# A transformer tower on one core: values', maxima's and query/key work reordered in the back end of each half, biases as a weight row, maxima taken in pairs

## The reference

```python
h = layer_norm(emb_word[ids] + emb_pos)
for l in range(4):                       # "token layers"
    q, k, v = h @ Wq + bq, h @ Wk + bk, h @ Wv + bv     # 12 heads of 16
    a = band_attention(q, k, v, mask)    # tokens within +-64
    h = layer_norm(h + a @ Wo + bo)
    h = layer_norm(h + gelu(h @ W1 + b1) @ W2 + b2)
# then one causal layer with rotary q/k, a shared expert, and top-2 of 16 experts
```

## Time and profile before

| | |
|---|---|
| median of 3 runs | 7051.08 us (7049.91 to 7069.48) |
| the profiled execution | 7050.01 us, its span 7048.2 us |
| mean granted TensorE clock | 0.939 |
| busy over the span | PE 86%, DVE 60%, ACT 32%, POOL 16% |
| token layers | from about 170 to 4640 us of the span |
| causal layer | from about 4640 to 5860 us |
| choice and experts | from there to the end |

### The profile page before, as it was taken

The page is one execution under the profiler, slowest core; times in us unless marked ns, Lnnn a source line. Parts: engine busy times, 40 slices in busy tenths (PEclk is TensorE's granted clock), DMA queues, the critical chain, the costliest instruction groups (busy, mean ns, idle before and its releaser), DMA issues. The chain is left out here.

```text
span 7048.2 us, 128877 instructions
## 1 busy us (share of the span) xinstructions
PE 6042.4 (86%) x46786; PEld 4744.2 (67%) x46786; DVE 4250.6 (60%) x11172; ACT 2239.1 (32%) x4196; POOL 1101.6 (16%) x1089
## 2 busy tenths in 40 slices
PE   1999999999999999999999999978888883289999
PEld 0777777777777777777777777756666662266766
DVE  6666666666666666666666666666666664722222
ACT  0333333333333333334333333323333330011111
POOL 5011111111111111111111111111111110234333
PEclk9999999999999999999999999989999986699999
DMA  6322223323232322222332232332222320033322
GB/s 119 62 60 60 60 61 65 70 61 66 58 64 60 75 61 60 60 60 60 67 70 61 62 65 60 65 69 56 62 64 63 64 56 10 1 84 73 88 69 55
DMA packets 1204450, 441.09 MB, mean 63 GB/s; under 512 B 1050338, under 2 KB 1191044, under 8 KB 1204324
## 3 DMA queue, kind: packets, MB, share of 16 engines
q1 hardware_dynamic: 1176676, 402.69, 26.7%
q0 software_dynamic: 27648, 36.72, 3.4%
HBM read 124.23 MB, written 60.26 MB: 26 GB/s over the span
## 5 line engine op out<-in xcount | busy, mean ns | idle before, releaser
L673 ACT ACTIVATE pT<-bank 128x384 f32<-128x384 f32 x1920 | 907.9, 490 | 872.8 <-PE bank L511 872.8
L843 DVE TENSOR_REDUCE mx<-bank 128x2 f32<-128x384 f32 x1548 | 802.2, 554 | 322.0 <-PE bank L483 285.1
L582 PE MATMUL bank<-hT,w 96*128 96x256 f32 x3072 | 848.0, 442 | 85.9 <-ACT hT L688 85.9
L582 PEld LDWEIGHTS bank<-hT,w 96*128 96x128 f32 x3072 | 678.6, 224 | 236.2 <-ACT hT L688 118.2
L509 PE MATMUL bank<-maskb,eyeb 128*128 128x384 bf16 x1920 | 635.1, 331 | 78.6 <-ACT pT L673 73.3
L481 PE MATMUL bank<-maskb,eyeb 128*128 128x384 bf16 x1932 | 634.5, 328 | 39.9 <-DMA qkT<-stack 20.7
L483 PE MATMUL bank<-qkT 128*128 128x192 bf16 (+2 forms) x3864 | 636.5, 247 | 0.0
L511 PE MATMUL bank<-qkT 128*128 128x192 bf16 (+2 forms) x3840 | 630.9, 246 | 0.0
L993 DVE TENSOR_TENSOR hout<-bank,resid 128x384 f32<-128x384 f32 x128 | 71.3, 557 | 769.4 <-PE bank L594 769.4
L594 PE MATMUL bank<-w,pT 128*128 128x192 f32 x3072 | 520.4, 326 | 0.0
L1022 POOL TENSOR_TENSOR rstd<-ve,half 128x2 f32<-128x2 f32 x160 | 127.7, 798 | 2486.6 <-DVE ve L749 2486.6
(11 more groups left out here) (197 smaller groups left out, 10230.5 us busy)
## 6 DMA issues: line engine op xcount, KB each, us to landing
hcur<-hbuf SPq DMA_DIRECT2D x165, 192.0 KB, 2.4
hbuf<-hout SPq DMA_DIRECT2D x128, 192.0 KB, 2.0
amb<-am_d SPq DMA_DIRECT2D x131, 128.0 KB, 2.9
exp_wg<-in_ewg SPq DMA_DIRECT2D x16, 768.0 KB
exp_wu<-in_ewu SPq DMA_DIRECT2D x16, 768.0 KB
exp_wd<-in_ewd SPq DMA_DIRECT2D x16, 576.0 KB
xs<-xr SPq DMA_DIRECT2D x32, 272.0 KB, 2.2
hbuf<-emb_z SPq DMA_DIRECT2D x17, 384.0 KB
```

The source lines that it names most:

```text
L582: last = nc.tensor.matmul(bank[s][f // 2][:, (f % 2) * S:(f % 2 + 1) * S], w1[:, c, f * P:(f + 1) * P], hT[s][:, c, :], start=(c == 0), st ...
L673: ph.inc(nc.scalar.activation(pT[s][:, h % NPT, :], bank[s][h % 2][:, 0:SCOLS], ACT.Exp, scale=SCALE), "p", s)
L843: last = nc.vector.tensor_reduce(mx[s][:, :, h], src[:, 0:SCOLS].rearrange("p (t k) -> p t k", t=T), AX, ALU.max)
```

## The change

TensorE's order after the scores is now: hidden transposes (into bank 0 of the stream, after the fifth pair of maxima), unkept, output, **V's values** (into bank 0 of F's stream), attention transposes, **the first bank of maxima** (bank 3), projection, q/k product (banks 1 and 2), **the second and third bank of maxima** (bank 0, and bank 2 of K's stream), h1's transposes, up- and down-projection; the up-projection's fifth block (third in the causal layer) waits for all row copies. The first scores use four banks in turn and VectorE reduces two heads in one instruction. The biases of q, k and v are a 97th row of the weights, with a row of ones below the hidden state, so nothing is added behind the product: ScalarE copies the values, and in the token layers the upper bf16 part of q/k straight from PSUM to `stack` (`act_top`), VectorE only takes the difference (`dve_rest`); in the causal layer ScalarE copies q/k. VectorE's row copies are split the same way as the maxima.

```diff
-        bank = [[ctx.enter_context(nc.psum_tensor(f"bank{s}{i}", [P, 512], F32)) for i in range(4)] for s in ST]
-        wqk = sb("wqk", [DC, 2, 2 * D], F32)
-        wv = sb("wv", [DC, 2, D], F32)
+        banks = [ctx.enter_context(nc.psum_tensor(f"banks{s}", [P, 4, 512], F32)) for s in ST]
+        bank = [[banks[s][:, i, :] for i in range(4)] for s in ST]
+        wqk = sb("wqk", [DC + 1, 2, 2 * D], F32)
+        wv = sb("wv", [DC + 1, 2, D], F32)
...
         def pe_hidden_T(ph, pe, G, F, causal):
             s = G.s
             if F:
-                ph.wait(pe, "y" if causal else "r2", F.s, F.it, 0)
+                ph.wait(pe, "mx", F.s, F.it, 5)
             ph.wait(pe, "x0" if causal else "h_in", s, G.it)
-            ph.inc(pe_transposes((h1 if causal else hcur)[s], bank[s][3]), "hT_ps", s)
+            ph.inc(pe_transposes((h1 if causal else hcur)[s], bank[s][0]), "hT_ps", s)
...
         def pe_qk(ph, pe, G, F):
             if F:
-                ph.wait(pe, "mT", F.s, F.it)
+                ph.wait(pe, "mx", F.s, F.it)
...
-                    last = nc.tensor.matmul(bank[s][t][:, 0:2 * D], hTa[s][:, c, t * P:(t + 1) * P],
-                                            wqk[:, c, :], start=(c == 0), stop=(c == 1))
+                    last = nc.tensor.matmul(bank[s][1 + t][:, 0:2 * D], hTa[s][rows_of(c), c, t * P:(t + 1) * P],
+                                            wqk[rows_of(c), c, :], start=(c == 0), stop=(c == 1))
...
         def pe_scores1(ph, pe, F, h, masks, qcols, causal):
-            if h >= 3:
-                ph.wait(pe, "mx", s, F.it, h - 2)
-            dst = bank[s][h % 3]
+            if h == 3:
+                ph.wait(pe, "y" if causal else "r2", s, F.it, 0)
+            if h >= 4 and h % 2 == 0:
+                ph.wait(pe, "mx", s, F.it, h // 2 - 1)
+            dst = bank[s][h % 4]
...
+        def maxima_bank(F, f):
+            return (bank[F.s][3], bank[F.s][0], bank[1 - F.s][2])[f]
+        def pe_maxima(ph, pe, F, V, K, f):
+            s = F.s
+            if f == 0:
+                ph.wait(pe, "m", s, F.it)
+            if f == 1 and V:
+                ph.wait(pe, "v", V.s, V.it)
+            if f == 2 and K:
+                ph.wait(pe, "att", K.s, K.it)
+            dst = maxima_bank(F, f)[:].bitcast(BF16)
...
             if K:
                 pe_output(ph, pe, K)
-            if F:
-                pe_maxima(ph, pe, F)
+            if V:
+                pe_v(ph, pe, V, G, F)
             if K:
                 pe_att_T(ph, pe, K)
-            if V:
-                pe_v(ph, pe, V, G)
+            if F:
+                pe_maxima(ph, pe, F, V, K, 0)
             if K:
                 pe_project(ph, pe, K)
             if G:
                 pe_qk(ph, pe, G, F)
+            if F:
+                pe_maxima(ph, pe, F, V, K, 1)
+                pe_maxima(ph, pe, F, V, K, 2)
             if K:
                 pe_h1_T(ph, pe, K, xr if causal else h1)
                 for f in range(FSC if causal else FC):
+                    if F and f == (2 if causal else 4):
+                        ph.wait(pe, "mT", F.s, F.it)
                     (pe_shared_up if causal else pe_up)(ph, pe, K, f)
...
+        def act_v(ph, act, V, K, causal):
+            s = V.s
+            ph.wait(act, "v_ps", s, V.it)
+            if K:
+                ph.wait(act, "otT_ps", K.s, K.it)
+                if not causal:
+                    ph.wait(act, "u_ps", K.s, K.it)
+            ph.inc(nc.scalar.copy(vaug[s][:, :, :, 0:DH],
+                                  bank[1 - s][0][:, 0:2 * D].rearrange("p (t h d) -> p t h d", t=T, h=NH)), "v", s)
+        def act_top(ph, act, G):
+            s = G.s
+            ph.wait(act, "xp", s, G.it, 0)
+            for t in range(T):
+                ph.wait(act, "qk_ps", s, G.it, t + 1)
+                ph.inc(nc.scalar.copy(stack[s][:, t].rearrange("p s h (m d) -> p (s h) m d", d=DH)[:, :, 0, :],
+                                      bank[s][1 + t][:, 0:2 * D].rearrange("p (x d) -> p x d", d=DH)), "qh", s)
...
             if G:
                 ph.wait(act, "hT_ps", G.s, G.it)
-                ph.inc(nc.scalar.copy(hTa[G.s][:], bank[G.s][3][0:DC, :]), "hT", G.s)
+                ph.inc(nc.scalar.copy(hTa[G.s][0:DC], bank[G.s][0][0:DC, :]), "hT", G.s)
+            if V:
+                act_v(ph, act, V, K, causal)
             if K:
                 ph.wait(act, "aT_ps", s, K.it)
                 ph.inc(nc.scalar.copy(hT[s][:], bank[s][3][0:DC, :]), "aT", s)
+            if G:
+                (act_qk if causal else act_top)(ph, act, G)
...
+        def dve_rest(ph, dve, G):
+            s = G.s
+            for t in range(T):
+                ph.wait(dve, "qh", s, G.it, t + 1)
+                ph.inc(nc.vector.tensor_tensor(
+                    rem[s][:, t].rearrange("p s h d -> p (s h) d"),
+                    bank[s][1 + t][:, 0:2 * D].rearrange("p (x d) -> p x d", d=DH),
+                    stack[s][:, t].rearrange("p s h (m d) -> p (s h) m d", d=DH)[:, :, 0, :], ALU.subtract), "qk", s)
...
             if qcols is BAND_COLS:
-                last = nc.vector.tensor_reduce(mx[s][:, :, h], src[:, 0:SCOLS].rearrange("p (t k) -> p t k", t=T),
-                                               AX, ALU.max)
+                last = nc.vector.tensor_reduce(mx[s][:, :, at].rearrange("p t h -> p h t"),
+                                               src[:, :, 0:SCOLS].rearrange("p h (t k) -> p h t k", t=T), AX, ALU.max)
...
             if F:
-                dve_maxima_rows(ph, dve, F)
-            if V:
...
-                dve_v(ph, dve, V)
+                dve_maxima_rows(ph, dve, F, (0,))
...
-            if G:
-                dve_qk(ph, dve, G)
+            if F:
+                dve_maxima_rows(ph, dve, F, (1, 2))
+            if G and not causal:
+                dve_rest(ph, dve, G)
...
-                    sp.dma_start(vqk[:], a["vec"][bass.ds(l, 1), 0:2 * D].to_broadcast([P, 2 * D])).then_inc(w_qk, 16)
...
-                    sp.dma_start(vv[:], a["vec"][bass.ds(l, 1), 2 * D:3 * D].to_broadcast([P, D])).then_inc(w_v, 16)
```

More of the change, by code:

```diff
@@ L466, in pe_v @@
                 for c in range(2):
-                    last = nc.tensor.matmul(bank[1 - s][3][:, t * D:(t + 1) * D], hTa[s][:, c, t * P:(t + 1) * P],
-                                            wv[:, c, :], start=(c == 0), stop=(c == 1))
+                    last = nc.tensor.matmul(bank[1 - s][0][:, t * D:(t + 1) * D], hTa[s][rows_of(c), c, t * P:(t + 1) * P],
+                                            wv[rows_of(c), c, :], start=(c == 0), stop=(c == 1))
             ph.inc(last, "v_ps", s)
@@ L485, in pe_scores1, with pe_scores2 @@
             ph.inc(last, "sc1", s)
-        def pe_maxima(ph, pe, F):
+        def maxima_bank(F, f):
+            return (bank[F.s][3], bank[F.s][0], bank[1 - F.s][2])[f]
+        def pe_maxima(ph, pe, F, V, K, f):
             s = F.s
[L490 to L495, removed]
-                                                   mrow[s][:, t, f * 4 + j, :], eyeb[:], tile_position=(0, DC))
-                ph.inc(last, "mT_ps", s)
-        def pe_scores2(ph, pe, K, V, h, masks, kcols):
+            if f == 0:
[5 more added lines that the diff above has]
+            dst = maxima_bank(F, f)[:].bitcast(BF16)
+            for j in range(4):
+                for t in range(T):
+                    last = nc.tensor.transpose(dst[DC:P, j * S + t * P:j * S + (t + 1) * P],
+                                               mrow[s][:, t, f * 4 + j, :], eyeb[:], tile_position=(0, DC))
+            ph.inc(last, "mT_ps", s)
+        def pe_scores2(ph, pe, K, V, F, h, masks, kcols):
             s = K.s
@@ L503, in pe_scores2 @@
                 ph.wait(pe, "qk", V.s, V.it)
+            if h == 0 and F:
+                ph.wait(pe, "v", F.s, F.it)
             if h == 0:
@@ L519, in pe_products @@
                 ph.wait(pe, "v", s, K.it)
-            if g == 2 and F:
-                ph.wait(pe, "v", F.s, F.it)
             ph.wait(pe, "p", s, K.it, 4 * g + 4)
@@ L660, in tensor_half, with act_qk @@
                 for f in range(FSC if causal else FC):
+                    if F and f == (2 if causal else 4):
+                        ph.wait(pe, "mT", F.s, F.it)
                     (pe_shared_up if causal else pe_up)(ph, pe, K, f)
                 (pe_shared_down if causal else pe_down)(ph, pe, K)
+        def act_v(ph, act, V, K, causal):
[14 more added lines that the diff above has]
+                                      bank[s][1 + t][:, 0:2 * D].rearrange("p (x d) -> p x d", d=DH)), "qh", s)
+        def act_qk(ph, act, G):
+            s = G.s
+            for t in range(T):
+                ph.wait(act, "qk_ps", s, G.it, t + 1)
+                ph.inc(nc.scalar.copy(qk[s][:, t].rearrange("p s h d -> p (s h d)"), bank[s][1 + t][:, 0:2 * D]), "qk", s)
         def scalar_half(ph, act, G, V, F, K):
@@ L919, in vector_half @@
             if F:
-                for h in range(NH):
```

(15 more changed lines are left out.)

74 lines of the change are left out of this document (33 added, 41 removed).

## The result

The changed kernel takes 6879.8 us (median of 4 runs, 6872.5 to 6881.1) where the kernel before, run beside it, takes 7050.5 (7048.5 to 7069.5): a ratio of 0.975, interval 0.973 to 0.977. The forecast was 6775 us, range 6700 to 6890: the sign is right and the time lies in the range, but at its upper end. 275 us were predicted, 171 came.

What follows compares the result with a forecast made beforehand. TensorE was taken to bound the kernel, losing time to idle and a falling clock. Token order 60, token clock 155, causal order 15 and causal clock 45 us sum to 275: 7050 to 6775 us, range 6700 to 6890.

Steps and rivals of the forecast that it cites:

- The token clock: Token layers: filling the idle around h1's transposes stops the clock falls, 1.22 us a half, 155 us in all.
- Rival C: Maxima's transposes don't hold the clock behind the q/k matmuls; only the order's 75 us are won: 6975 us; chance 0.10.
- Rival B: Token clock falls come half as often, at the attention's new opening or where waits turn out longer: 6853 us; chance 0.20.
- The token order: Token halves: the projection starts sooner behind the attention's transposes, 0.47 us a half, 60 us over 128 halves.
- The causal layer: Causal layer: 15 us from the order in 32 halves, and 45 us from half of the clock's loss back.
- The 97th row: Bias row in the weights: matmuls costed at nothing, bounded by 6 us; its transfers lie under whole halves.
- a wait of the hidden state's transposes: End of the scores: transposes wait for the fifth pair of maxima, 0.2 us if a pair takes 1.11, 25 us over 128 halves.
- D: Slower: clock falls at the attention's opening too, as often as before at h1's, beside Rival C's falls: 7130 us; chance 0.04.
- E: Openings stay as long, through ScalarE or the row copies, and the clock with them: within 20 us of 7050; chance 0.04.
- ScalarE's copies: Values' copy and two `stack` halves on ScalarE: no cost, or up to 0.5 us a half if h1's copy waits.
- the maxima in pairs: Scores on VectorE: a two-head reduction taken at 0.95 us, between 0.90 and 1.11; the last pair ends about when it did.
- the bias additions: VectorE: the values' addition goes, two bias additions become two subtractions of the same size; no time counted.

Runs made afterwards that it cites:

- the maxima first: Changed kernel with all three banks of maxima ahead of the projection, none behind the q/k product: 7111.1 us, ratio 1.013 to the kernel before.
- the added transposes: Changed kernel with all three maxima banks ahead of the projection, plus 16 unread narrow transposes behind the token layers' q/k product: 7004.6 us, ratio 0.998.

## Why the prediction came out as it did

**The token clock: right.** 155 us predicted; the clock's loss there went from 151.9 us to nothing. Its argument held too: with 1.6 to 1.8 us of idle around h1's transposes the clock fell in 68 of 127 halves before and in 43 with the maxima first, with 0.7 to 1.0 us it never did. Rival C (these transposes don't hold it; 0.10) falls with the added transposes. Rival B's place, the attention's opening, is real: with the three banks behind q/k it fails in 55 of 127 halves, at 1.4 to 1.7 us of idle and at 1.5 about as often as at 1.7; with one bank in it, at 0.9 to 1.2 us, in none. So the 0.20 for it was not idle caution. Between 1.2 and 1.4 us nothing was measured.

**The token order: right in kind, sized 0.47 us a half, measured 0.33.** Undisturbed halves are (33.06 + 33.34)/2 = 33.20 against 33.54. The projection starts 1.39 us after the attention's transposes in the half shown, in alternate halves 1.31 as predicted: 0.04 on average. The other 0.10 is the projection's own matmuls, 1.40 us to the next group instead of 1.30. The sum took them over from the earlier trace rows, where they follow other matmuls without a wait; in the new place their first one takes 0.10 us more. Why stays open; one guess was tested and fell. 128 x 0.14 = 18 us. With clock and order this stretch gained 190.8 us of 215.

**The causal layer: wrong, 60 us predicted and none won.** The step that failed is the sentence "POOL's first rotary half in the causal layer can start earlier", costed at nothing. I took an earlier start on an engine off the critical path as harmless and asked only whether its queue or its waits would hold anyone. It slows the engine beside it instead, on the path: VectorE's normalisation took 1.42 us more a half, which undid the order's gain there and widened the opening before xr's transposes to 1.70 us (1.27 in the earlier trace rows), and most of the clock's loss stayed (85 of 104 us; the prediction had put the 104 at some 90). With the rotation late the layer gives 70 us: 51 us less of clock than in the kernel before, against 45 predicted, and 18 us of order, against 15.

**The 97th row: wrong for the first load.** I costed its matmuls and put the transfers under whole halves. That holds for all loads but the first, under which nothing lies: 8.6 us to the first up-projection, of which the separate row gives back 7.5.

**The rest:** the time lies in the range, but by a way that the range was not built on: its upper end, 6890, was B with half of the token falls left and a wait of the hidden state's transposes. What filled it was the causal layer, the order's smaller size, the first load and the 10 us in the choice and the experts. That 6880 is inside is in part luck. Of the changed kernel neither D nor E holds; D's place, the attention's opening, does fall once its bank of transposes is gone.

**What was costed at nothing and was nothing:** ScalarE's copies, the maxima in pairs, the bias additions, the bank order. Only the pairs were tested alone. For the others the token halves leave no room: 0.43 us sooner at the projection less 0.10 in it is the 0.33 measured.

## What to carry to other kernels

Work that must be done anyway and waits for nobody belongs in the openings of TensorE's path, split so that each opening gets some: three banks at one place gave ratios of 1.013 or 0.995 to the kernel before, one and two gave 0.975. When a change lets an engine start earlier, look at what runs beside it at the new time, not only at who waits for it; a wait put in on purpose was worth 70 us here. And look at the first pass of every load apart from the others, since here nothing covered it.

## What was not expected of the hardware

- POOL's tensor operations on SBUF make VectorE's f32 scalings from SBUF to SBUF take 701 instead of 376 ns (192 columns) and 692 instead of 307 ns (64 columns): nearly the same time for a third of the columns, so it looks as if they wait for POOL's instruction rather than run at a lower rate. That reading is argued, not shown.
- While a load of 97 rows ran, the core's transfers together made 18 GB/s; with the same rows as 96 and one, 197 (215 with 96 rows before).
- Added transposes made a kernel 108 us faster in the token layers, by the clock alone.
- The first matmul of a group took 0.10 us more to the next one where the group waited for its input (320 against 216 ns in the up-projection) or came behind narrow transposes (267 against 162 in the projection).
- One reduction over two PSUM banks costs 957 ns against 2 x 554.
